# Two transformer layers on one core: separate transposed q and k for the second batch, the shared expert's tiles in the first batch's place, another order of steps

## The reference, cut to what matters

```python
x = layernorm(x + L0_attn(x))  # retention: 8 heads of 32, rotated q and k, decay mask, group norm, gate
x = layernorm(x + L0_ffn(x))   # ternary weights, sigmoid(x w1) * (x w2), then w3; inner width 704
x = layernorm(x + L1_attn(x))  # causal softmax attention, 16 heads of 16, 512 tokens a batch
x = layernorm(x + L1_ffn(x))   # shared expert (inner width 704) + 2 of 8 experts per token (inner width 176)
```

```python
scores = einsum('bhtd,bhsd->bhts', q, k) * scale
probs = softmax(scores + causal, axis=-1)
y = einsum('bhts,bhsd->bhtd', probs, v)
```

## Time and profile before

| | |
|---|---|
| median of 3 runs | 442.24 us (442.02 to 443.8) |
| the profiled execution, its own time | 439.05 us |
| its span, first to last instruction | 437.2 us |
| TensorE (PE) busy | 351.0 us, 80% |
| VectorE (DVE) busy | 308.1 us, 70% |
| ScalarE (ACT) busy | 221.8 us, 51% |
| GpSimd (POOL) busy | 178.2 us, 41% |
| mean granted TensorE clock | 0.948 of full |

### The profile page before, as it was taken

One profiled execution on the slowest core, in us unless ns is written; L12 is line 12 of the kernel. 1 busy time (PEld: TensorE's weight loads), 2 busy tenths in 40 slices (PEclk: granted clock), 3 DMA queues, 4 the chain that ended last, 5 costly groups with the idle time before them and its releaser, 6 DMA issues.

```text
span 437.2 us, 8262 instructions
## 1 busy us (share of the span) xinstructions
PE 351.0 (80%) x2700; PEld 199.5 (46%) x2700; DVE 308.1 (70%) x807; ACT 221.8 (51%) x464; POOL 178.2 (41%) x216
## 2 busy tenths in 40 slices
PE   0887778778797798789787888877898989999890
PEld 0354556554565333343463333334565544555460
DVE  4664678756798973663699878665888786586635
ACT  4594754457254347888731287742424344554510
POOL 3265676555430025433200036831215463437643
PEclk9996999799999999999897699987999999999996
DMA  7999998111001000153100000223002124352241
GB/s 235 320 265 224 225 222 247 42 41 50 0 2 49 0 1 2 54 165 94 49 1 1 0 3 27 72 74 100 26 1 74 62 75 123 92 151 73 85 132 62
DMA packets 25981, 38.53 MB, mean 88 GB/s; under 512 B 2258, under 2 KB 21266, under 8 KB 25938
## 3 DMA queue, kind: packets, MB, share of 16 engines
q1 hardware_dynamic: 23732, 31.93, 27.8%
q0 software_dynamic: 2208, 6.07, 3.9%
HBM read 30.88 MB, written 17.49 MB: 111 GB/s over the span
## 4 chain that ended last, share of the span: by engine, by line
PE 43%; DVE 19%; issue 7%; ACT 6%; POOL 2%; SPq 2%; DMA 1%; POOLq 0%; DVEq 0%; ACTq 0%
DVE arena_mixers L1334 7%; PE psum_a L616 6%; PE psum_a L894 5%; PE psum_a L863 5%; PE psum_a L908 5%; PE psum_a L753 4%; PE psum_b L825 2%; PE psum_b L616 2%; ACT arena_mixers L1064 2%; PE psum_b L765 2%; PE psum_a L815 2%; PE psum_b L901 1%; SPq L553 1%; DVE cut_weights L1170 1%; PE psum_b L882 1%
## 5 line engine op out<-in xcount | busy, mean ns | idle before, releaser
L1548 POOL TENSOR_TENSOR ln_rstd<-ln_var_eps,minus_half 128x1 f32<-128x1 f32 x32 | 22.7, 709 | 78.0 <-DVE ln_var_eps L1161 78.0
L616 PE MATMUL psum_a<-cut_weights,x_transposed 128*128 128x512 f16 (+1 forms) x210 | 38.6, 334 | 13.8 <-DVE cut_weights L1170 12.6
L1334 DVE TENSOR_REDUCE arena_mixers<-psum_a 128x2 f16<-128x768 f32 (+3 forms) x44 | 47.0, 1124 | 0.9 <-PE psum_a L799 0.7
L1064 ACT ACTIVATE arena_mixers<-psum_a 128x1024 f32<-128x1024 f32 (+2 forms) x48 | 40.6, 885 | 7.9 <-PE psum_a L815 7.6
L1537 POOL DMA_INDIRECT expert_out<-block_out,arena_ffn x30 | 29.6, 988 | 31.2 <-ACT block_out L1115 27.5
L1565 POOL TENSOR_SCALAR_AFFINE_SELECT arena_mixers<-arena_mixers 128x256 f32<-128x256 f32 (+1 forms) x48 | 24.1, 513 | 34.6 <-ACT arena_mixers L1064 34.4
L894 PE MATMUL psum_a<-cut_weights,stage 128*128 x180 | 32.0, 314 | 6.1 <-issue 5.5
L863 PE MATMUL psum_a<-x_transposed,cut_weights 128*128 128x512 f16 (+1 forms) x144 | 34.8, 394 | 0.7 <-issue 0.3
L616 PEld LDWEIGHTS psum_a<-cut_weights,x_transposed 128*128 128x128 f16 x210 | 19.9, 104 | 29.4 <-DVE cut_weights L1170 13.2
L1553 POOL TENSOR_TENSOR arena_ffn<-arena_ffn 128x512 f16<-128x512 f32 (+1 forms) x12 | 14.0, 1178 | 41.6 <-ACT arena_ffn L1034 41.6
L825 PE MATMUL psum_b<-arena_mixers 128*32 128x512 f32 (+3 forms) x256 | 24.2, 457 | 6.9 <-POOL arena_mixers L1565 5.3
(11 more groups left out here) (251 smaller groups left out, 836.7 us busy)
## 6 DMA issues: line engine op xcount, KB each, us to landing
expert_in<-in_row_init SPq DMA_DIRECT2D x1, 10140.0 KB, 51.1
stage<-in_wexp SPq DMA_DIRECT2D x9, 512.0 KB, 3.6
arena_ffn<-expert_in SPq DMA_DIRECT2D x30, 130.0 KB, 2.1
stage<-in_wsh SPq DMA_DIRECT2D x5, 437.0 KB, 10.7
arena_mixers<-expert_out SPq DMA_DIRECT2D x16, 128.0 KB, 2.3
arena_ffn<-in_w SPq DMA_DIRECT2D x1, 1408.0 KB, 7.2
stage<-in_xT SPq DMA_DIRECT2D x2, 512.0 KB, 4.3
stage<-in_wqkvg SPq DMA_DIRECT2D x2, 512.0 KB, 5.3
```

Source lines behind the costliest of these rows:

```text
L616: ins = mm(dst, lhs[k][a], rhs(k, b, col), start=(k == 0 and a == 0 and b == 0), stop=(bias_at is None and k == n - 1 and a == 1))
L1064: ins = nc.scalar.activation(heads, by_row_tile(ps, se_heads(j))[:, :, :, 0:w], ACT.Exp, scale=1.0 / 16)
L1334: v.tensor_reduce(ST[:, i, 0, h0:h0 + n_h, 48].rearrange("p (h s) -> p s h", s=2), by_row_tile(ps, n_h)[:, :, :, 0:(i + 1) * P], AX.X, ALU ...
L1548: g_.tensor_tensor(rstd[:, r:r + 1], veps[:, r:r + 1], half[:, 0:1], ALU.pow).then_inc(ln_rstd[layer], 1)
```

## The change

1. QT and KT become lists of two: batch 0's lie where they lay, batch 1's at the end of arena2, behind the blocks' tables. The readers and writers (tq, tm, mx, se) index them by batch.
2. HTS and HS, the shared expert's tiles, move from the beginning of arena2 to the place of batch 0's QT and KT in arena1.
3. In `dependences`, tq of batch 1 no longer needs the last se of batch 0, but the last dn (layer 0 FFN), whose tiles lie under the new ones. The last pv of each group of four of batch 1 needs the last ya of batch 0. rb needs the last dn.
4. ORDER is another list of the same 599 steps, with other PSUM tiles. No instruction is added, removed or changed in shape, and no load is added.

The code, cut:

```diff
-            add(("tq", b, i), ("qk", b, i), at(b, ("se", 0, AH // 4 - 1, TB - 1, 0)))
+            add(("tq", b, i), ("qk", b, i), at(b, ("dn", NT - 1)))
...
-                add(("pv", b, g, j), ("se", b, g, j, 4 - se_heads(j)))
+                add(("pv", b, g, j), ("se", b, g, j, 4 - se_heads(j)), at(b and j == TB - 1, ("ya", 0, TB - 1)))
...
-        add(("rb", b), ("rc", b * TB + TB - 1))
+        add(("rb", b), ("rc", b * TB + TB - 1), ("dn", NT - 1))
...
-        QT = cut([AH // 2, TB * P], f16)
-        KT = cut([AH // 2, TB * P], f16)
+        heads_at = cut.at
+        QT, KT = ([cut([AH // 2, TB * P], f16)] for _ in range(2))
...
-        cut = Carve(arena2)
+        cut = Carve(arena1)
+        cut.at = heads_at
         HTS = cut([2, FM, TB * P], f16)
         HS = cut([2, TB * P])
+
+        cut = Carve(arena2)
         XB = cut([2 * GROUP, ROW])
...
+        QT.append(cut([AH // 2, TB * P], f16))
+        KT.append(cut([AH // 2, TB * P], f16))
...
-                        ins = mm(out_of[:, h % 2, h // 2, 0:(i + 1) * P], QT[r:r + 64, p, i * P:(i + 1) * P],
-                                 KT[r:r + 64, p, 0:(i + 1) * P], start=False, stop=True, skip_group_check=True)
+                        ins = mm(out_of[:, h % 2, h // 2, 0:(i + 1) * P], QT[b][r:r + 64, p, i * P:(i + 1) * P],
+                                 KT[b][r:r + 64, p, 0:(i + 1) * P], start=False, stop=True, skip_group_check=True)
```

More of the change, by code:

```diff
@@ L97 @@
 ORDER = """
[L98 to L112, removed]
@@ L128 @@
-    bd:a2 bt:b0 bd:a0 bt:b1 bd:a2 bd:a1 fin ln3 sd:a0 sd:a2 sd:b1 sd:a0 os os fin os fin os ln3 fin ln3 fin ln3
-    ln3
+    cen bias split cen split cen split split split proj:a0 rot pg:a1 pg:a2 proj:a0 split split split tqk:b0 wsum
+    kv:b1 proj:a1 rot rot sc:a2 sc:a0 wsum proj:a1 ret:b1 tqk:a2 vr:b0 proj:a2 tqk:b1 sc:a1 sc:a2 wsum sc:a0 kv:b0
+    rot rx:b1 yg yh kv:a1 rot tqk:b0 ret:a2 sc:a0 sc:a1 vr:b0 gsum:a2 wo0:b1 proj:a0 quant ln0 ret:b1 sc:a1 tqk:b0
+    vr:b0 rx:a1 sc:a0 quant yg tx0:b1 proj:a1 ret:b0 vr:a2 quant rx:a0 yg rot proj:a1 bias tqk:b0 yh rx:b0 yg sc:a2
@@ new lines @@
+    sc:a1 kv:a0 yh rot sc:a2 split ret:b1 wo0:b0 wo0:b1 yh split vr:b1 ret:b0 kv:a0 rot ln0 wo0:a1 rx:a0 yg ln0 ln0
+    tqk:b1 sc:a1 tqk:b0 sc:a2 sc:a1 tx0:a0 yh vr:b0 kv:b1 sc:a1 wo0:a2 ret:b0 tx0:a0 tx0:a1 rx:b1 vr:a2 up:a0 split
+    cut up:a1 up:a2 cut cut up:a0 rx:b0 yg yg up:a2 cut yh yh cut up:a1 ret:b1 cut wo0:b0 vr:a1 dn:b1 dn:a1 ln1 ln1
+    rx:b1 yg tx1:a0 dn:b0 tx1:a2 yh ln1 ln0 dn:b0 tx1:b0 ln0 split wo0:a2 wo0:b1 ln1 tx0:b0 ln0 qk:a0 qk:a1 tx1:b0
+    qk:a2 tq:a1 ln0 split tx0:a0 qk:a2 tq:a0 tq:a1 mx:a2 mx:a0 mx:a2 tq:a1 tm:b0 mx:a0 mx:a1 mx:a0 mx:a2 mx:a1 mx:a2
@@ new lines @@
+    tx0:b0 mx:a0 mx:a1 mx:a2 tm:b0 mx:a0 mx:a1 mx:a2 mx:a0 tm:b1 tx0:a1 mx:a2 mx:a0 up:a1 up:a2 cut mx:a0 cut up:a1
+    mx:a2 cut up:a0 cut mx:a1 mx:a2 up:a0 tm:a1 cut se:a1 se:a2 up:a0 pv:b1 cut se:a1 se:a2 se:a0 dn:b0 ln1 pv split
+    se:a1 split pv se:a2 tx1:b0 pv se:a0 dn:a1 dn:b1 pv:b0 se:a2 split se:a1 se:a0 ln1 ln1 qk:a2 tx1:b1 pv pv se:a1
+    split tx1:b1 se:a2 se:a0 split pv qk:a1 qk:a0 se:a2 pv:b0 se:a1 dn:b1 se:a2 pv se:a0 ln1 tx1:a2 pv se:a1 pv
+    se:a2 split qk:a0 split se:a0 pv:b0 se:a2 se:a1 split pv se:a0 split pv tq:a2 split tq:a0 tq:a2 mx:a1 mx:a0 pv
@@ new lines @@
+    tq:a1 mx:a2 ya:b1 ya:a0 mx:a2 mx:a0 ty:b0 ya:b1 ty:a1 mx:a2 mx:a1 mx:a2 mx:a0 mx:a1 wo2:a2 ya:b0 mx:a1 mx:a0
+    mx:a2 ty:b1 ln2 mx:a0 tm:b0 mx:a2 wo2:a1 mx:a0 ty:a2 mx:a1 tm:b0 mx:a2 mx:a0 mx:a1 mx:a2 mx:a0 wo2:b0 ln2 tm:b1
+    tm:a1 wo2:b1 ln2 ln2 se:a0 se:a1 tx2:b1 tx2:b0 se:a2 se:a0 pv:b1 se:a1 rt:b0 pv se:a1 tx2:a2 tx2:b0 rt:a0 pv pv
+    se:a2 rc se:a1 rc su:a0 se:a1 rt:b1 pv:b0 se:a2 se:a2 pv se:a2 rk:b1 pv sx se:a0 rt:b1 se:a2 pv se:a0 rk:b0 sx
+    sh rc rc se:a1 su:a2 sh rk:b0 pv:b1 se:a0 pv se:a2 sx rk:a0 su:a1 pv se:a0 sx rb:b0 pv se:a2 se:a0 se:a1 su:a2
```

36 lines of the change are left out of this document (16 added, 20 removed).

## The result

The changed kernel took 445.85 us in the median of 11 runs (443.50 to 446.93), the one before 442.02 beside it (436.30 to 444.94). The ratio is 1.014, with an interval from 1.009 to 1.018: slower, by 3.8 us between the medians and 6 us by the ratio, outside my range (433.0 to 444.5) and on the other side. Ratios here compare undisturbed executions alone, medians are over all runs; where few runs were taken the two can differ (e9: ratio 0.988, quotient of medians 0.995), and then I lean on neither alone.

What follows compares the result with a forecast made beforehand. No engine was taken as full, TensorE nearest, so the stage decides. Start 0, into maxima 0, out of them -0.4, handover -3.6 sum to -4.0 us: 442.24 - 4.0 = 438.2 us, range 433.0 to 444.5.

Steps and rivals of the forecast that it cites:

- Tiles at nothing, no use made of them: Batch 1's transposes: new tiles cost nothing, and the new order doesn't use the freedom to make them during batch 0's scores.
- Start, 0, between -2.3 and +2.1: Start of the kernel: earlier splits of pieces 4 to 7 taken as 0, kept between -2.3 and +2.1 us.
- The rival in which ScalarE is late: Start: ScalarE cuts pieces 5 to 7 first, delaying what follows, and the handover gains nothing; 445.0 us, chance 0.17.
- Into batch 1's maxima, 0: Ahead of batch 1's first maximum: at most 0.70 us idleness won, at most 1.06 lost, taken as 0.
- out of them, -0.4: End of batch 1's maxima: the last tm on TensorE can start at once behind the last maximum, -0.4 us.
- the sign of a loss in layer 0: Batch 1's maxima beginning over 2 us later than 216.9 would put the loss in layer 0.
- Handover, -3.6: From attention into the experts, 287 to 308 us: fewer waits and less half clock, -3.6; at best -6.9, at worst nothing.
- (b): Handover: bi 5 moved later no longer holds VectorE waiting for blocks 5 to 9, sparing TensorE's wait, -1.53 us.
- (a): Handover: the last pv go ahead, so TensorE's second wait for the blocks' rows is covered, -0.76 us.
- (c): Handover: half of the 2.60 us that su 5 and ya's transposes lose at half clock is regained, -1.30 us.
- Layer 0, "can't price", 2 us either way: Layer 0's shuffled steps, not priced singly: an eighth of its 16.1 us TensorE idleness, 2 us either way.
- The block loop, 2 us either way: Shuffled steps outside layer 0, not priced singly: 2 us either way; after 308 us, gains won ahead are kept.

Runs made afterwards that it cites:

- e9: The changed kernel with sx 5 (two indirect DMAs on GpSimd) moved from directly behind sx 4 to behind bd 7; ratio to before 0.988, 0.995 by the medians.
- e1: Before's order, step by step, with the changed kernel's tiles; ratio to before 1.001.
- e2: Before with only its first 63 steps (the start) in the new order, before's tiles; ratio to before 1.000.
- e7: Before with steps 320 to 459 (first scores of batch 1 through the handover to the experts) in the new order; ratio 0.995 [0.992, 0.999].
- e5: The changed kernel's whole order with before's tiles; ratio to before 1.006, interval 1.002 to 1.010.
- e15: e8 with before's order in steps 320 to 459 too, except bi 5 moved behind bu 4; ratio to before 0.993.
- e11: The new order with before's tiles, but steps 63 to 160 (layer 0) in before's order; ratio to before 1.001.
- e8: Before's tiles, new order in steps 0 to 62 and 161 to 459, before's order elsewhere; median 436.54 us, ratio to before 0.990.
- e14: e11 with sx 5 moved behind bd 7; ratio to before 0.990 [0.983, 0.996].
- e6: The changed kernel with one layer 0 step, bias 1, moved from behind proj 7 to behind wo 0.2; ratio to before 1.017.
- e13: The changed kernel with two layer 0 steps moved, bias 1 behind wo 0.2 and tqk 6 behind split 8; ratio to before 1.015.
- e10: e8 with sx 5 moved directly behind sx 4, making six indirect DMAs in a row; ratio to before 0.996.
- e4: Before with its last 139 steps (behind bu 9) in the new order, before's tiles; ratio to before 1.011, four runs.

## Why the prediction was wrong

I forecast -4.0 us and measured +3.8. The gain that I priced came; two terms that I had left as allowances of 2 us either way, around 0, turned the sign. By its own steps:

- **Tiles at nothing, no use made of them:** right (e1).
- **Start, 0, between -2.3 and +2.1:** right as measured (e2: 1.000). The rival in which ScalarE is late did not happen; its sign in the profile (A) is, if anything, the other one.
- **Into batch 1's maxima, 0; out of them, -0.4:** the first maximum of batch 1 ends at 220.7 (218.1 before), 2.5 us late. I had named this as the sign of a loss in layer 0, and that is what it is. The -0.4 came: the last tm begins 0.05 us behind the last maximum (250.01, 249.96) where it was 0.46. D gains 1.4 us between the two profiled executions; the ranges of the two orders only touch (81.1 to 83.6, 80.3 to 81.2). The first se of batch 1 is 1.2 us later than before, just over the 1 us that I had given it.
- **Handover, -3.6:** the mechanisms were right, and the sum met -3.4 in F by luck. Against the other profiles of the old handover F gained 5.2 to 6.5 us, and in time the whole part was worth 2 us (e7). (b) bi 5 was sized 1.53 us; alone it gave 3.1 us at bu 3 and 1.5 at bu 9 against before's profile, but 3.4 to 4.6 at bu 9 against the four others. So of the 2.7 us that I took for covered by su 5 a part wasn't. (a) and (c) are the rest: no wait for the rows, and full clock. Here the chip sides with the rule of the Trainium skill ("TensorE: Matmul & The Clock Gate", section "What's actually happening"), that activity releases full speed: 1.00 with TensorE busy 18.96 us of 21, where I had taken half. I left out E and G, which took back a part in e7 (0.9 and 1.4 us): E took 0.9 us longer in e7 and e5, 1.8 in the changed kernel, though before's order has a 40.6 too (e15).
- **Layer 0, "can't price", 2 us either way:** the first step that failed. It lost 4.5 us in the profiles (B and C), about 0.5% in time (e5 to e11). I took idle time for the measure of what could change (an eighth of 16.1 us); in B, what changed was the granted clock, at which the same 226 matmuls took 4.8 us more than in before and 6.3 more than in e8.
- **The block loop, 2 us either way, "what is won ahead of it is kept":** the second step that failed, and the larger. G lost 4.7 us, and up to 7 between kernels (e11 to e14). It is one edit: sx 5 directly behind sx 4. I had counted loads and their queue for SP, and not the DMAs of GpSimd's sx. Even so I would have priced it as two issues of 1.27 us earlier on an engine that is busy 40%, and not as TensorE's signals held up, of which before's trace has only faint signs (0.45 us behind a row of three).

Of the rivals, "the start is late" (0.17) came nearest, 445.0 us against 445.85, and by luck: its start costs nothing (e2) and the handover, which it had gain nothing, gained. None named either mechanism.

What stays open: which steps of layer 0 bring the half clock (e6 and e13 moved the two nearest to its waits, and it came elsewhere), why the profile makes layer 0 twice as dear as the times do, and by what path GpSimd's DMAs hold TensorE's signals. That the row of DMAs is the cause is shown by taking two of its six away (e9, e14) and adding them (e10); the path is not. What costs 1.8 us in C, and e4's 1.011, stay open too.
